# A Fourier mixing layer on one core: weights loaded a stage earlier, their signs turned on GpSimd, a reordered first cycle, shared copies and a flip that reads in runs

## The reference

```
xf = rfft2(x, axes=(1, 2), norm='ortho')            # 128 x 65 frequencies, 8 blocks of 96 channels
o1r = relu(xr @ w1[0] - xi @ w1[1] + b1[0])         # per block, 96 x 96
o1i = relu(xi @ w1[0] + xr @ w1[1] + b1[1])
o2r = o1r @ w2[0] - o1i @ w2[1] + b2[0]
o2i = o1i @ w2[0] + o1r @ w2[1] + b2[1]
o = sign(o2) * max(abs(o2) - 0.01, 0)               # softshrink of both parts
out = irfft2(o, s=(128, 128), norm='ortho') + x
```

## Time and profile before

| | us |
|---|---|
| median of 3 runs (lowest, highest) | 5054.24 (5045.23, 5054.70) |
| profiled execution, its own time | 5048.19 |
| its span | 5046.4 |
| TensorE busy (share of the span) | 4878.2 (97%) |
| VectorE busy | 3829.9 (76%) |
| ScalarE busy | 3005.9 (60%) |
| GpSimd busy | 1511.3 (30%) |

### The profile page before, as it was taken

How to read it: one execution, slowest core, us unless ns; L and a number is a source line. 1 busy time by engine, 2 the same in 40 slices (tenths; PEclk the granted TensorE clock), 3 DMA queues, 4 the chain that set the end, 5 groups by cost and what they waited for, 6 DMA issues and landing times.

```text
span 5046.4 us, 113165 instructions
## 1 busy us (share of the span) xinstructions
PE 4878.2 (97%) x40000; PEld 4718.3 (93%) x40000; DVE 3829.9 (76%) x6159; ACT 3005.9 (60%) x5409; POOL 1511.3 (30%) x905
## 2 busy tenths in 40 slices
PE   6999999999999999999999999999999999999997
PEld 6999999999999999999999999999999999999996
DVE  5777777777777777777777777777777778777776
ACT  4556665556655566655566555665556665556653
POOL 3033223332233322233322333223332223332230
PEclk8999999999999999999999999999999999999998
DMA  5044333444234442334433344423444233443333
GB/s 115 1 106 106 74 70 83 94 106 91 59 79 91 106 106 64 70 85 102 106 75 74 79 93 106 88 64 77 91 106 96 66 70 87 106 106 75 74 77 88
DMA packets 1699718, 430.28 MB, mean 85 GB/s; under 512 B 1698848, under 2 KB 1698976, under 8 KB 1699104
## 3 DMA queue, kind: packets, MB, share of 16 engines
q1 hardware_dynamic: 1696768, 421.83, 37.9%
q10 hardware_dynamic: 2336, 0.59, 0.1%
HBM read 220.84 MB, written 201.33 MB: 84 GB/s over the span
## 4 chain that ended last, share of the span: by engine, by line
PE 74%; SPq 12%; DVE 7%; issue 4%; DMA 2%; ACT 0%; DVEq 0%; ACTq 0%
PE psum L807 13%; PE psum L892 13%; PE psum L822 10%; PE psum L853 9%; PE psum L876 8%; SPq L373 8%; PE psum L839 5%; PE psum L870 5%; SPq L398 4%; PE psum L902 3%; PE psum L903 3%; PE psum L904 3%; DMA b_rows<-L_conv_b 2%; DVE mixed L686 2%; DVE spectrum L694 1%
## 5 line engine op out<-in xcount | busy, mean ns | idle before, releaser
L573 ACT ACTIVATE sums_high<-psum 128x512 fp32r<-128x512 f32 x768 | 457.9, 598 | 722.5 <-PE psum L892 722.5
L533 ACT ACTIVATE excess<-psum,over 128x768 f32<-128x768 f32 (+1 forms) x544 | 481.4, 885 | 645.9 <-PE psum L876 534.5
L822 PE MATMUL psum<-w_whole,whole 128*128 128x192 f32 x4160 | 797.5, 335 | 33.4 <-ACT whole L496 12.0
L853 PE MATMUL psum<-mats,mixed 128*128 128x128 f32 x6272 | 761.0, 276 | 57.0 <-DVE mixed L686 57.0
L853 PEld LDWEIGHTS psum<-mats,mixed 128*128 128x128 f32 x6272 | 739.0, 192 | 74.1 <-DVE mixed L686 74.0
L822 PEld LDWEIGHTS psum<-w_whole,whole 128*128 128x128 f32 x4160 | 685.4, 197 | 97.1 <-issue 70.9
L686 DVE COPY mixed<-psum 128x768 f32<-128x768 f32 (+1 forms) x512 | 475.3, 928 | 392.0 <-PE psum L822 308.1
L876 PE MATMUL psum<-w2t,hidden 128*128 128x192 f32 x4160 | 763.0, 327 | 0.0
L892 PE MATMUL psum<-mats,spectrum 128*128 128x128 f32 x6144 | 744.3, 275 | 5.3 <-DVE sums_low L748 4.6
L807 PEld LDWEIGHTS psum<-mats,x 128*128 128x128 f32 x6144 | 702.9, 193 | 41.7 <-issue 16.3
L807 PE MATMUL psum<-mats,x 128*128 128x128 f32 x6144 | 708.1, 276 | 33.1 <-DVE x L614 17.2
(11 more groups left out here) (76 smaller groups left out, 7453.3 us busy)
## 6 DMA issues: line engine op xcount, KB each, us to landing
x<-x SPq DMA_DIRECT2D x736, 192.0 KB, 2.8
out<-x SPq DMA_DIRECT2D x736, 192.0 KB, 2.5
x<-x SPq DMA_DIRECT2D x736, 64.0 KB, 2.6
out<-x SPq DMA_DIRECT2D x736, 64.0 KB, 2.2
x<-x SPq DMA_DIRECT2D x32, 144.0 KB, 2.7
out<-x SPq DMA_DIRECT2D x32, 144.0 KB, 2.3
w2t<-L_conv_w SPq DMA_DIRECT2D x124, 36.0 KB, 1.8
x<-x SPq DMA_DIRECT2D x64, 48.0 KB, 2.3
```

Source lines behind the costliest of these rows:

```text
L822: last = pe.matmul(bank_b(s, k), whole[s % 2][:, k // 2, :, k % 2], w1_whole[par][:, :, :].rearrange("p r o -> p (r o)"), start=opens and ...
L853: last = pe.matmul(out[tile], flat[:, tile * SIZE:(tile + 1) * SIZE], mat(FH), start=True, stop=True)
```

## The change

1. `load_w` goes ahead of the stores in SyncE's loop and waits for the unit's last stage D instead of following store piece 0.
2. `prepare_step` is gone from VectorE. GpSimd's new `negate` does the six signs, after `halve` of the unit before and ahead of its own fold. VectorE instead waits for the weights at the start of its layers.
3. In the first cycle TensorE takes whole 0, halved 0, halved 1, whole 1, and ScalarE gathers halved 1 before whole 1.
4. The last two groups of stage A (22, 23) are copied by both engines: ScalarE the rows, VectorE the third.
5. `real_kw` is laid out with the 96 channels innermost, so the flip's moving operand is read in runs of 96; `shrink` writes it with a stride.
6. In unit 0 ScalarE copies all of groups 0 to 17, and VectorE only folds until then.

```diff
+A_SHARED = [NA - 2, NA - 1]
...
-        real_kw = sb("real_kw", [SIZE, BLOCK, 6])
+        real_kw = sb("real_kw", [SIZE, 6, BLOCK])
...
                 for par in range(2):
+                    sp.wait_ge(d_done, (m * 2 + par + 1) * NS)
+                    load_w(sp, m + 1, par)
                     for p in range(NP + 1):
...
-                        if p == 0:
-                            load_w(sp, m + 1, par)
...
+            def negate(m, par):
+                unit = m * 2 + par
+                pool.wait_ge(w_loaded[par], (m + 1) * W_LOADS * 16)
+                parts = [(w1_whole[par][BLOCK:SIZE, 0], BLOCK, SIZE), (w1_halved[par][:, 0], 0, SIZE)]
+                parts += [(w2t[par][lo:hi, col:col + BLOCK], lo, hi) for lo, hi, col in NEGATED]
+                for k, (part, lo, hi) in enumerate(parts):
+                    pool.tensor_tensor(part, part, minus[lo:hi, :].broadcast_to([hi - lo, BLOCK]), ALU.mult).then_inc(w_negated, 1)
+                    pool.wait_ge(w_negated, unit * W_SIGNS + (k + 1))
...
+            negate(0, 0)
             halve(0, 0)
+            pool.wait_ge(x_halved, 1)
+            negate(0, 1)
             fold(0, 1)
             with pool.Fori(1, PAIRS) as m:
...
                     halve(m * 2 + par - 1, 1 - par)
+                    pool.wait_ge(x_halved, m * 2 + par)
+                    negate(m, par)
                     fold(m, par)
...
+                for at in range(NA - 2):
+                    if at not in A_ACT and not (first and at < EARLY):
+                        continue
...
+                for at in A_SHARED:
+                    act.wait_ge(a_done, n * NA + (at + 1))
+                    act.activation(evict_views(A_ORDER[at])[0], bank_a(at)[0:BLOCK].rearrange("p (s j) -> p s j", s=A_ROWS),
+                                   ACT.Copy).then_inc(act_copied, 1)
...
                 act.wait_ge(w_loaded[par], (m + 1) * W_LOADS * 16)
+                gather_halved(1)
                 gather_whole(1)
-                gather_halved(1)
...
-            def prepare_step(m, par, k):
...
+                for at in A_SHARED:
+                    dve.wait_ge(a_done, n * NA + (at + 1))
+                    dve.tensor_copy(evict_views(A_ORDER[at])[1], bank_a(at)[BLOCK:].rearrange("p (s j) -> p s j", s=A_ROWS)).then_inc(dve_copied, 1)
...
-                dst = real_kw[:, :, :] if t == REAL else U[:, 0:BLOCK, j:j + rows]
+                dst = real_kw[:, :, :].rearrange("p r c -> p c r") if t == REAL else U[:, 0:BLOCK, j:j + rows]
...
+            for i in range(NP):
+                fold_first(i)
+            forward(0, True)
+            layers(0, 0, 0, True)
...
-                pe.matmul(bank_flip, mat(FLIP_RE), real_kw[:, :, 0::4].rearrange("p c k -> p k c"), start=True, stop=False)
+                pe.matmul(bank_flip, mat(FLIP_RE), real_kw[:, 0::4, :], start=True, stop=False)
...
-                for s in PAIRED[0]:
-                    stage_b_whole(par, n, s, True)
-                for s in PAIRED[0]:
-                    stage_b_halved(par, n, s, False)
+                stage_b_whole(par, n, 0, True)
+                stage_b_halved(par, n, 0, False)
+                stage_b_halved(par, n, 1, True)
+                stage_b_whole(par, n, 1, False)
```

More of the change, by code:

```diff
@@ L108, in sum_rows @@
     return spread[:SPREAD // 2] + own + last
-A_ACT = [at for at in range(NA) if at % 2 == 0 or at == NA - 3]
-A_DVE = [at for at in range(NA) if at not in A_ACT]
+A_SHARED = [NA - 2, NA - 1]
+A_ACT = [at for at in range(NA - 2) if at % 2 == 0 or at == NA - 3]
+A_DVE = [at for at in range(NA - 2) if at not in A_ACT]
+ACT_COPIES, DVE_COPIES = len(A_ACT) + len(A_SHARED), len(A_DVE) + len(A_SHARED)
 EARLY = 18
@@ L204, in fourier_mlp @@
         over = sb("over", [SIZE, 1])
-        half = sb("half", [SIZE, 1])
+        half, minus = sb("half", [SIZE, 1]), sb("minus", [SIZE, 1])
         b1t = [sb(f"b1t{i}", [SIZE, 3]) for i in range(2)]
@@ L460, in halve @@
                                    ALU.mult).then_inc(x_halved, 1)
+            def negate(m, par):
[6 more added lines that the diff above has]
+                    pool.wait_ge(w_negated, unit * W_SIGNS + (k + 1))
             pool.memset(half[:, :], 0.5).then_inc(half_set, 1)
-            pool.wait_ge(half_set, 1)
+            pool.memset(minus[:, :], -1.0).then_inc(half_set, 1)
+            pool.wait_ge(half_set, 2)
+            negate(0, 0)
             halve(0, 0)
+            pool.wait_ge(x_halved, 1)
+            negate(0, 1)
             fold(0, 1)
@@ L511, in gather_halved, with forward @@
                 act.activation(h[HALF:SIZE], parts[0:HALF, 1, 1], ACT.Copy).then_inc(halved_gathered, 1)
-            def forward(n):
-                for at in A_ACT:
+            def forward(n, first=False):
+                for at in range(NA - 2):
+                    if at not in A_ACT and not (first and at < EARLY):
+                        continue
                     act.wait_ge(a_done, n * NA + (at + 1))
                     src = bank_a(at).rearrange("p (s j) -> p s j", s=A_ROWS)
-                    rows, third = evict_views(A_ORDER[at])
-                    act.activation(rows, src[0:BLOCK], ACT.Copy)
-                    act.activation(third, src[BLOCK:], ACT.Copy).then_inc(act_copied, 1)
+                    views = evict_views(A_ORDER[at])
+                    if len(views) == 3:
+                        act.activation(views[0], src[0:BLOCK, 0:A_ROWS - 1], ACT.Copy)
+                        act.activation(views[1], src[0:BLOCK, A_ROWS - 1:], ACT.Copy)
+                    else:
+                        act.activation(views[0], src[0:BLOCK], ACT.Copy)
+                    copied = act.activation(views[-1], src[BLOCK:], ACT.Copy)
+                    if at in A_ACT:
+                        copied.then_inc(act_copied, 1)
+                    else:
+                        copied.then_inc(dve_copied, 1)
+                for at in A_SHARED:
+                    act.wait_ge(a_done, n * NA + (at + 1))
+                    act.activation(evict_views(A_ORDER[at])[0], bank_a(at)[0:BLOCK].rearrange("p (s j) -> p s j", s=A_ROWS),
+                                   ACT.Copy).then_inc(act_copied, 1)
             def rectify(par, n, t):
@@ L538, in layers @@
                 act.wait_ge(u_zeroed, n + 2)
-                act.wait_ge(act_copied, (n + 1) * len(A_ACT))
-                act.wait_ge(dve_copied, (n + 1) * len(A_DVE))
+                act.wait_ge(act_copied, (n + 1) * ACT_COPIES)
+                act.wait_ge(dve_copied, (n + 1) * DVE_COPIES)
                 gather_whole(0)
                 act.wait_ge(w_loaded[par], (m + 1) * W_LOADS * 16)
+                gather_halved(1)
                 gather_whole(1)
-                gather_halved(1)
                 for j, pair in enumerate(PAIRED):
@@ L583, in _ @@
             load_w(act, 0, 0)
-            forward(0)
+            forward(0, True)
             layers(0, 0, 0)
@@ L600, in _, with fold_first @@
             dve.tensor_tensor(iw_low[:, :, :], iw, iw_high[:, :, :], ALU.subtract).then_inc(iw_split, 1)
-            t = xs[0]
-            for i, (lo, hi) in enumerate(PIECES):
+            def fold_first(i):
+                t, (lo, hi) = xs[0], PIECES[i]
                 up, down = t[:, lo:hi + 1, :], mirrored(t, lo, hi)
@@ L649, in forward @@
-            def forward(n):
+            def forward(n, first=False):
                 dve.memset(U[0:BLOCK, 0:HALF + 1, SIZE + 2:SIZE + 4], 0.0).then_inc(u_zeroed, 1)
                 for at in A_DVE:
[L652 to L660, removed]
+                    if not first or at >= EARLY:
+                        dve.wait_ge(a_done, n * NA + (at + 1))
+                        src = bank_a(at).rearrange("p (s j) -> p s j", s=A_ROWS)
+                        views = evict_views(A_ORDER[at])
+                        if len(views) == 3:
+                            dve.tensor_copy(views[0], src[0:BLOCK, 0:A_ROWS - 1])
+                            dve.tensor_copy(views[1], src[0:BLOCK, A_ROWS - 1:])
+                        else:
+                            dve.tensor_copy(views[0], src[0:BLOCK])
+                        dve.tensor_copy(views[-1], src[BLOCK:]).then_inc(dve_copied, 1)
@@ L661, in forward @@
                     if at in (EARLY - 1, EARLY + 1):
-                        dve.wait_ge(act_copied, n * len(A_ACT) + EARLY // 2)
-                        dve.wait_ge(dve_copied, n * len(A_DVE) + EARLY // 2)
+                        dve.wait_ge(act_copied, n * ACT_COPIES + EARLY // 2)
+                        dve.wait_ge(dve_copied, n * DVE_COPIES + EARLY // 2)
                         lo, hi = (0, INNER[0]) if at < EARLY else (INNER[1], SIZE)
@@ L670, in forward @@
                             dve.tensor_copy(halved[0][y * HALF:(y + 1) * HALF, lo:hi], parts[0:HALF, 1, y])
-                dve.wait_ge(act_copied, (n + 1) * len(A_ACT))
-                dve.wait_ge(dve_copied, (n + 1) * len(A_DVE))
+                for at in A_SHARED:
```

(23 more changed lines are left out.)

## The result

The changed kernel takes 4919.43 us (median of 4917.82, 4919.26 and 4919.61) against 5049.73 of the kernel before, run beside it: a ratio of 0.9743, interval 0.973 to 0.9756. The forecast was 4946 with a range of 4922 to 4978. The direction held, and each part of the change won at least what the forecast gave it; the gain was 129 us of span (5046.4 to 4917.5) where the sum had said 104. One further execution of the changed kernel, 6371.93 us long at a mean granted clock of 0.73, is left out.

The account below looks back on a forecast made before the run. TensorE, working 97% of the span, was taken as the bound. Opening 25, signs 44, copies 10, first cycle 10 and flip 15 sum to 104 us, from 5050.6 to 4946, range 4922 to 4978.

Parts of the forecast that it names:

- Opening: Unit 0 up to its first stage C: ScalarE's copies set the pace, C starts at 51.4 not 77.49; gain 25 us.
- The signs: Steady layers: VectorE's waits for late weights and its slow signs stall TensorE; moving them to GpSimd gains 44 us.
- the price on TensorE: TensorE's 57.0 us of waits on `mix`, less the first cycle's, 41.6, plus 3.2 for `L870`: 44.8 us.
- The early load: Weights issued ahead of store piece 0: pixels come some 2 us earlier, no price, no gain.
- both causes: VectorE's wait for the last weight transfer, and its signs slowed while the fold runs on GpSimd; both leave VectorE.
- First cycle: First stage B to first C: halved 0 in second place lets `mix` begin earlier; 0.33 x 31 = 10 us (6 to 13).
- its 0.48: First cycle: TensorE's 0.48 us wait for `mix` of group 0, within 4.86 us from first B to first C.
- Flip: Before stage E: reads in runs save 0.70 us, last `shrink` caps it at 0.56; 0.5 x 31 = 15 us.
- a sign of being wrong: Stage E waiting for `shrink` in most units would show the forecast wrong.
- the `shrink` that I feared to be late: Last `shrink` before stage E, possibly held up by the unfold step ahead in some units, leaving less than 0.56 us.
- Copies: End of stage A: sharing the last copies starts the gather 0.43 us earlier; 25 x 0.42 = 10 us (7 to 11).
- The rivals: Blocked steps return: 4968, 0.14; opening at 1.2 GHz: 4964, 0.09; flip hidden: 4961, 0.10; fold late, slower: 5256, 0.03.

Follow-up runs that it names:

- the run with 12 fills: Changed kernel with VectorE held up in its cycle 5 by 12 small waited-for fills of a scratch tile, some 4 us in all: 5014.4 us (0.9922 of before).
- the late load: Changed kernel with the weights loaded behind store piece 0 again: 4921.60 us, 0.9745 of before.
- old copies: Changed kernel with stage A's last two copies each on one engine again: 0.9775 of before.
- the old flip: Changed kernel with the flip's old `real_kw` layout and old strided reads: 0.9791 of before.

## Why the prediction was wrong

- **Opening: right.** 26.2 us against 25. ScalarE's pace was the limit as worked out, and the clock did not drop on the way (granted 1.00 from 16 to 55 us).
- **The signs: mechanism right, price too low.** The step that failed is "the price on TensorE is the 57.0 us of the earlier trace rows less the 32 waits of 0.48 us": 44.8, taken as 44 with 46 as its upper bound, where the stretch gave 56.6. The time of a stall was read from the matmul row. A wait there is counted from the modelled end of the matmul before, and it leaves out the slow start after the stall: 0.16 and 0.10 us a stall in the run with 12 fills. In the unit with the longest stretch of before (90.57, 3.94 above the rest) the two rows read:

```profile
PE psum L853 <- DVE mixed L686: 3.1, 2, 2.3
PE psum L870 <- DVE psum L708: 0.3, 1, 0.3
...
PEld psum L853 <- DVE mixed L686: 3.5, 2, 2.5
...
PEld psum L870 <- DVE psum L708: 0.6, 1, 0.6
```

  The weight loads' row (PEld) gives 4.1, of which 0.2 for `L870` stands in undisturbed units too: 3.9; the matmul row gives 3.4. Over the 32 units the weight loads' idle time in this stretch (gaps over 0.15 us, as the list of waits counts them) fell from 126.9 to 73.3, 53.6 us, and the matmuls' from 45.7 to 0.8, 44.9. The stretch fell by 56.6, and with VectorE held up by 12 fills the three stood in the same order: 2.25, 2.44, 2.52. This is half of the miss of 25 us; first cycle and flip, each 5.3 us above the forecast and above their upper bounds too (13 and 20), are most of the rest.
- **The early load: right, neither price nor gain.** The forecast put the gain on both causes leaving VectorE, and the kernel with the signs alone on GpSimd shows that moving them is enough.
- **First cycle: mechanism right, 13.6 us of 31 x 0.44 in place of 10**, since its 0.48 was a wait of the matmul row as well. By the starts, the first stage C came 0.80 us after the last matmul of B before and comes 0.16 after it now: 0.64 won. The one more change between whole and halved cost 0.20 and not 0.15. Another 1.7 are one clock drop fewer behind the loop's jump.
- **Flip: mechanism right, 20.3 in place of 15.** That E is bound by the last `shrink` is true: in all units it starts 0.05 or 0.06 us after it, where before it was 0.70 in most. The forecast had named this as a sign of being wrong; it came, and costs little, since the flip is 0.68 us shorter (1.33 to 0.65) and E comes 0.64 earlier. The start takes 0.05 and not 0.14, and the `shrink` that I feared to be late in some units is late in none of this trace; in the runs with the late load and the old copies it was, in four and two units. `shrink` into `real_kw` did become dearer by its stride, which I had at nothing, and stayed hidden (0.76 us before):

```profile
L720 DVE SCALAR_TENSOR_TENSOR real_kw<-psum,excess 128x576 f32<-128x576 f32 x32 | 38.0, 1189 | 15.8 <-ACT excess L567 15.8
```

- **Copies: right**, 10.3 against 10.
- **The rivals**: none came. GpSimd's signs took 0.34 to 0.35 us each in the steady part, `L664` and `L669` (the unfold) are as long as before, and behind unit 0 no stage A waited for a fold.

The Trainium skill's warning (Perfetto Trace Analysis, section Optimizing Scalar/DVE Operations) that moving work between VectorE and GpSimd might not help did not come true here: the 57 us stayed won, perhaps since in the steady part the products run beside instructions of VectorE that read or write PSUM (`seed`, `mix`, the clips). That is read from the timeline and was not tested by a run: with the late load they ran some 50 us later in the unit, also without a cost, but beside such instructions again. That the two block each other the trace bears out, with the 3.02 us in place of 0.44 of the earlier trace rows and the 9.7 us that the signs cost when they stayed on VectorE with their weights in time.

## What to carry to other kernels

Price a stall of TensorE by the distance between starts, or by the idle time of its weight loads; the matmul row's own waits begin at a modelled end and missed a fifth here, about 0.25 us a stall. Work that waits for a transfer belongs on an engine whose queue has nothing urgent behind it: the wait for the late weights was 3.1 us a unit on VectorE and cost TensorE 47 us in all, and it was 50 us a unit on GpSimd and cost nothing. When an experiment of 0.3% is lost in the scatter between runs, cut every unit at the same starts and compare stretches: away from loop heads and clock drops most repeat to 0.02 us.

## What I had not expected of the hardware

- A strided moving operand cost TensorE twice the time here: 0.67 us a pair with 24 bytes between elements, 0.32 in runs of 96.
- A strided write cost VectorE as well: 1.19 us in place of 0.76 for 576 elements a partition with 384 bytes between neighbours, and 0.76 again in the run with the old flip.
- An idle stretch of 2.0 to 2.3 us of TensorE was followed by a stretch at the lower clock (granted 0.53 to 0.61), or not: of 32 equal stalls of 2.25 us on the matmul row ten were, at about 1.6 us each.
